# Gram matmuls of a DLRM tower, moved from blocks of their own to the places between other matmuls

## What is computed

```
e = jnp.stack([tbl_0[ids[:, 0]], ..., tbl_25[ids[:, 25]]], axis=1)
combined = jnp.concatenate([dense_features[:, None, :], sparse_features], axis=1)
interactions = jnp.einsum('bnd,bmd->bnm', combined, combined)
interactions_flat = interactions[:, _TRIU_I, _TRIU_J]
z = jnp.concatenate([dense_features, interactions_flat], axis=1)
h = jnp.concatenate([z, r_dense_features], axis=1)
h = jnp.maximum(h @ W_top1 + b_top1, 0.0)
h = jnp.maximum(h @ W_top2 + b_top2, 0.0)
y = h @ W_top3
```

## Time and profile before

| | |
|---|---|
| median of 3 runs | 381.85 us (380.86 to 382.14) |
| the profiled execution | 384.91 us, span 382.8 us |
| TensorE matmuls busy | 341.9 us (89%) |
| TensorE weight loads busy | 304.2 us (79%) |
| GpSimd busy | 252.1 us (66%) |
| VectorE, ScalarE busy | 193.2 us, 125.5 us |
| granted TensorE clock, mean | 0.99 of full |

### The profile page before, as it was taken

The page is one execution under the profiler, slowest core; times in us unless marked ns, Lnnn a source line. Parts: engine busy times, 40 slices in busy tenths (PEclk is TensorE's granted clock), DMA queues, the critical chain, the costliest instruction groups (busy, mean ns, idle before and its releaser), DMA issues.

```text
span 382.8 us, 13108 instructions
## 1 busy us (share of the span) xinstructions
PE 341.9 (89%) x6048; PEld 304.2 (79%) x6048; DVE 193.2 (50%) x94; ACT 125.5 (33%) x211; POOL 252.1 (66%) x267
## 2 busy tenths in 40 slices
PE   0788878984999999999999999999999999999995
PEld 0687767883898898898988898889988898977763
DVE  2899996565424396228833495238742595100000
ACT  2235433332132341334322342323322333343122
POOL 3777887777777777777777777777777777500200
PEclk9999999999799999999999999999999999999999
DMA  8975698254322537225632536234622533420400
GB/s 205 222 210 166 170 301 250 58 195 126 126 80 58 193 82 200 58 80 177 149 119 58 194 92 190 58 120 140 187 79 58 193 89 86 144 73 27 154 13 0
DMA packets 30868, 49.57 MB, mean 129 GB/s; under 512 B 17499, under 2 KB 17635, under 8 KB 30686
## 3 DMA queue, kind: packets, MB, share of 16 engines
q1 hardware_dynamic: 22350, 31.68, 27.0%
q0 software_dynamic: 8320, 16.92, 16.8%
q10 hardware_dynamic: 144, 0.13, 0.1%
HBM read 38.21 MB, written 10.49 MB: 127 GB/s over the span
## 4 chain that ended last, share of the span: by engine, by line
PE 72%; POOL 14%; issue 6%; DMA 4%; DVE 2%; ACT 1%; DVEq 0%
PE look_ps L309 28%; POOL rows L290 14%; PE mid_ps L339 13%; PE layer_ps L356 11%; PE layer_ps L365 7%; PE mid_ps L321 7%; PE layer_ps L353 4%; DMA rows<-in_table,index 3%; DVE match L463 2%; PE layer_ps L372 2%; DMA index<-in_index 1%; ACT hidden L528 0%; ACT hidden L534 0%; ACT turned L501 0%; ACT turned L512 0%
## 5 line engine op out<-in xcount | busy, mean ns | idle before, releaser
L290 POOL DMA_INDIRECT rows<-in_table,index x256 | 248.8, 972 | 82.3 <-issue 75.0
L463 DVE TENSOR_TENSOR match<-look_ids,row_number_ps 125x2048 fp32r<-125x2048 int32 x80 | 181.7, 2286 | 132.2 <-PE look_ps L309 122.3
L309 PE MATMUL look_ps<-match,table_high 125*128 125x256 f32 x640 | 165.7, 296 | 20.2 <-DVE table_low L471 18.1
L309 PE MATMUL look_ps<-match,table_low 125*128 125x256 f32 x640 | 159.4, 286 | 0.1
L309 PEld LDWEIGHTS look_ps<-match,table_high 125*128 125x128 f32 x640 | 124.8, 195 | 25.0 <-issue 16.0
L309 PEld LDWEIGHTS look_ps<-match,table_low 125*128 125x128 f32 x640 | 125.1, 195 | 0.0
L339 PEld LDWEIGHTS mid_ps<-turned 128*32 128x32 f32 x4096 | 45.3, 109 | 19.1 <-issue 15.3
L339 PE MATMUL mid_ps<-turned 128*32 128x27 f32 x4096 | 54.4, 195 | 5.5 <-issue 1.7
L501 ACT COPY turned<-look_ps 128x512 f32<-128x512 f32 x40 | 31.9, 798 | 73.5 <-PE look_ps L309 72.2
L508 ACT COPY turned<-mid_ps 128x512 f32<-128x512 f32 x64 | 42.8, 672 | 19.7 <-PE mid_ps L321 19.5
L321 PE MATMUL mid_ps<-identity,rows 128*128 128x128 f32 x256 | 40.6, 283 | 9.4 <-DMA rows<-in_table,index 8.5
(11 more groups left out here) (21 smaller groups left out, 44.8 us busy)
## 6 DMA issues: line engine op xcount, KB each, us to landing
look_ids<-in_look_rows SPq DMA_DIRECT2D x40, 256.0 KB, 4.4
scratch<-grams SPq DMA_DIRECT2D x8, 864.0 KB, 4.4
rows<-in_table,index POOLq DMA_INDIRECT x256
scratch<-grams SPq DMA_DIRECT2D x8, 416.0 KB, 5.2
pairs<-scratch SPq DMA_DIRECT2D x92, 29.2 KB
grams<-in_table SPq DMA_DIRECT2D x4, 448.0 KB
pairs<-in_table SPq DMA_DIRECT2D x3, 448.0 KB
hidden<-in_table SPq DMA_DIRECT2D x3, 448.0 KB
```

Of the source, the lines that this page charges most:

```text
L290: pool.indirect_dma_start(out=rows[j % 2][:, at, :], out_offset=None, in_=tables[GATHERED[at]], in_offset=bass.IndirectOffsetOnAxis(ap=ind ...
L309: last = nc.tensor.matmul(look_ps[pair % 2][:, r % 2, :], part[0:table_rows, r, c, :], match[number % 2][0:table_rows, c, :], start=(c == ...
L463: nc.vector.tensor_tensor(match[number % 2][0:table_rows], look_ids[b][0:table_rows, r % 2].unsqueeze(1).broadcast_to(shape), row_number_p ...
```

## The change

28 of the 32 gram steps (all but the four of the last group) lose their block. `look` takes a gram step along and sets four samples behind every matmul, or behind every second one (`every=2`); `layer1` and `layer2` take four samples behind each of their matmuls. In the main loop from g = 2, steps 0, 1 and 2 are half in a look and half in layer 1 or layer 2; step 3 stands whole in a look. The steps of group 0 and of group 6 stand whole in looks. The numbers of the shared PSUM banks follow the new order (each turn now ahead of its gram step), and so does ScalarE's order. In the last group's tail the blocks of gram and of the layers change places.

```diff
+            def look(g, r, step=None, every=1):
                 ...
+                if step is not None:
+                    gram_ready(g - 1, step)
                 for c in range(PARTS):
-                    for part in (table_high, table_low):
+                    for h, part in enumerate((table_high, table_low)):
                         last = nc.tensor.matmul(look_ps[pair % 2][:, r % 2, :], part[0:table_rows, r, c, :],
                         ...
-                last.then_inc(look_done, 1)
+                        if c == PARTS - 1 and part is table_low:
+                            last.then_inc(look_done, 1)
+                        if step is not None and (2 * c + h + 1) % every == 0:
+                            four_samples(g - 1, step, (2 * c + h) // every)
...
+            def four_samples(g, k, i):
+
+                x = k * IN_STEP + i
+                for s in range(QUADS):
+                    n = (x // BLOCK * P + s * BLOCK + x % BLOCK) * FEATURES
+                    last = nc.tensor.matmul(
+                        mid_ps[gram_number(g, k) % 3][s * ROW:(s + 1) * ROW, i * FEATURES:(i + 1) * FEATURES],
+                        turned[g % 2][:, n:n + ROW], turned[g % 2][:, n:n + FEATURES], start=True, stop=True)
+                if i == IN_STEP - 1:
+                    last.then_inc(gram_done, 1)
...
+            turn(1, 0)
+            look(1, 6, step=0)
...
-                gram(g - 1, 0)
-                turn(g, 0)
-                look(g, 6)
-                if g >= 2:
-                    layer1(g - 2, 0)
-                    layer1(g - 2, 1)
...
+                    turn(g, 0)
+                    look(g, 6, step=0, every=2)
+                    layer1(g - 2, 0, grams=(g - 1, 0, 8))
+                    layer1(g - 2, 1, grams=(g - 1, 0, 12))
...
+                    turn(g, 2)
+                    look(g, 8, step=2, every=2)
+                    layer2(g - 2, grams=(g - 1, 2, 8))
+                    turn(g, 3)
+                    look(g, 9, step=3)
                     layer3(g - 2)
...
             for k in range(STEPS):
-                gram(g - 1, k)
                 turn(g, k)
-                look(g, AHEAD + k)
+                look(g, AHEAD + k, step=k)
             layer1(g - 2, 0)
             layer1(g - 2, 1)
             gram(g, 0)
             layer1(g - 2, 2)
+            layer1(g - 2, 3)
             gram(g, 1)
...
+            layer2(g - 2)
+            for k in range(STEPS, TURNS):
+                turn(g, k)
             gram(g, 2)
-            layer2(g - 2)
+            layer3(g - 2)
             gram(g, 3)
-            layer3(g - 2)
```

More of the change, by code:

```diff
@@ L161, in pair_end, with mid_order @@
             return 2 * number + 2
-        PERIOD = TURNS + STEPS
-        def turn_number(g, k):
[L169 to L174, removed]
+        def mid_order():
+            yield from (("turn", 0, k) for k in range(TURNS))
+            for g in range(1, groups):
+                for k in range(STEPS):
+                    yield "turn", g, k
+                    yield "gram", g - 1, k
+                if g + 1 < groups:
+                    yield from (("turn", g, k) for k in range(STEPS, TURNS))
+            yield from (("gram", g, 0), ("gram", g, 1))
+            yield from (("turn", g, k) for k in range(STEPS, TURNS))
+            yield from (("gram", g, 2), ("gram", g, 3))
+        mid_place = {step: number for number, step in enumerate(mid_order())}
+        def turn_number(g, k):
+            return mid_place["turn", g, k]
         def gram_number(g, k):
[L177 to L180, removed]
+            return mid_place["gram", g, k]
         block = ctx.enter_context(nc.Block())
@@ L323, in turn, with gram_ready @@
                 last.then_inc(turn_done, 1)
-            def gram(g, k):
-                number = gram_number(g, k)
+            def gram_ready(g, k):
                 if k == 0:
@@ L333, in gram, with layer1 @@
                     pe.wait_ge(mid_out, turn_number(g, TURNS - 1) + 1)
-                after(pe, mid_out, number - 2)
-                for i in range(IN_STEP):
[L336 to L344, removed]
+                after(pe, mid_out, gram_number(g, k) - 2)
+            def four_samples(g, k, i):
[7 more added lines that the diff above has]
+                    last.then_inc(gram_done, 1)
+            def gram(g, k):
+                gram_ready(g, k)
+                for i in range(IN_STEP):
+                    four_samples(g, k, i)
+            def layer1(g, o, grams=None):
                 if o == 0 and g + 1 < groups:
@@ L354, in layer1 @@
                                  dense[:, g * N:(g + 1) * N], start=True, stop=False)
+                if grams is not None:
+                    four_samples(*grams)
                 for c in range(CHUNKS):
@@ L357, in layer1, with layer2 @@
                                             pairs[0:CHUNK_ROWS, g % 2, c, :], start=False, stop=(c == CHUNKS - 1))
-                if o % 2 == 1:
-                    last.then_inc(layer1_done, 1)
-            def layer2(g):
+                    if c == CHUNKS - 1 and o % 2 == 1:
+                        last.then_inc(layer1_done, 1)
+                    if grams is not None:
+                        of, k, first = grams
+                        four_samples(of, k, first + 1 + c)
+            def layer2(g, grams=None):
                 pe.wait_ge(hidden1_ready, L1 * (g + 1))
@@ L366, in layer2 @@
                                                 start=(c == 0), stop=(c == L1 - 1))
-                last.then_inc(layer2_done, 1)
+                        if o == L2 - 1 and c == L1 - 1:
+                            last.then_inc(layer2_done, 1)
+                        if grams is not None:
+                            of, k, first = grams
+                            four_samples(of, k, first + o * L1 + c)
             def layer3(g):
@@ L390, in _ @@
             pe.wait_ge(dense_in, 16)
+            turn(1, 0)
+            look(1, 6, step=0)
+            turn(1, 1)
+            look(1, 7, step=1)
+            turn(1, 2)
+            look(1, 8, step=2)
+            turn(1, 3)
+            look(1, 9, step=3)
             for g in range(1, groups - 1):
@@ L394, in _ @@
                     pe.wait_ge(weights_in, WEIGHT_DMAS)
-                gram(g - 1, 0)
-                turn(g, 0)
-                look(g, 6)
                 if g >= 2:
-                    layer1(g - 2, 0)
-                    layer1(g - 2, 1)
-                gram(g - 1, 1)
-                turn(g, 1)
-                look(g, 7)
-                if g >= 2:
[L405 to L410, removed]
-                    layer2(g - 2)
[L412 to L415, removed]
+                    turn(g, 0)
+                    look(g, 6, step=0, every=2)
+                    layer1(g - 2, 0, grams=(g - 1, 0, 8))
+                    layer1(g - 2, 1, grams=(g - 1, 0, 12))
+                    turn(g, 1)
+                    look(g, 7, step=1, every=2)
+                    layer1(g - 2, 2, grams=(g - 1, 1, 8))
+                    layer1(g - 2, 3, grams=(g - 1, 1, 12))
+                    turn(g, 2)
[3 more added lines that the diff above has]
+                    look(g, 9, step=3)
                     layer3(g - 2)
@@ L592, in _ @@
             g = groups - 1
+            take_turned(g, 0)
             take_gram(g - 1, 0)
-            take_turned(g, 0)
+            take_turned(g, 1)
             take_gram(g - 1, 1)
-            take_turned(g, 1)
             take_look(g, 3)
-            take_gram(g - 1, 2)
             take_turned(g, 2)
             put_dense(g)
+            take_gram(g - 1, 2)
+            take_turned(g, 3)
             take_gram(g - 1, 3)
-            take_turned(g, 3)
             take_look(g, 4)
@@ L605, in _ @@
             take_gram(g, 0)
+            relu1(g - 2, 1)
             take_gram(g, 1)
[L607 to L611, removed]
+            relu2(g - 2)
+            for k in range(STEPS, TURNS):
+                take_turned(g, k)
             take_gram(g, 2)
-            relu2(g - 2)
+            copy_y(g - 2)
             take_gram(g, 3)
-            copy_y(g - 2)
             for g in (groups - 2, groups - 1):
```

15 lines of the change are left out of this document (4 added, 11 removed).

## The result

The changed kernel takes 549.06 us in the median (545.08 to 551.04), the kernel before 381.93 us: 1.437 times as long, 95% interval 1.428 to 1.446. That is +167 us where +101 was forecast, and beyond the range's 525. The profiled execution took 550.15 us, with a span of 548.3 us.

What follows compares the result with a forecast made beforehand. From about 97 us TensorE's own queue was taken to bound the kernel, GpSimd's gathers close behind. Pieces 165.8, removed blocks -54.3, hidden -10 and -1, tail +0.4 made +100.9 us on the 381.85 median: 483 us, range 445 to 525.

Steps and rivals of the forecast that it cites:

- rival 2: Next wide weights load during the piece, so 0.11 us of its exit goes: 0.26 us a piece, 433 us; chance 5%.
- A piece: Four samples set among look or layer matmuls, entry, matmuls and exit together: 0.37 us each, 165.8 us for 448.
- The exit into a look: Passage from a piece's gram matmuls back to a look matmul, taken like layer 1's: 0.23 us.
- layer matmuls about 0.59 us: Sign of being right: layer matmuls on either side of a piece stand about 0.59 us apart.
- the clock falls: Spread pieces leave TensorE's array mostly empty; all at the lower level 703 us, a fifth 527; chance 7% beyond 525.
- A main-loop group: Sign of being right: TensorE's period of a main-loop group goes from 42.3 to 58.2 us.
- what is hidden: In group 0's stretch, 57 to 103 us, added grams fill idle time and end slow clock: 10 us off.
- VectorE's match waits: TensorE's waits for VectorE's matches go: another 1 us off.
- the tail: Layer 3 of group 5 moves ahead of the last gram and no longer covers the chain to pairs: +0.4 us.
- Rival 1: Pieces cost array time alone, spreading may avoid pauses inside blocks: -23 us, capped by gathers at about 369 us; chance 6%.

Runs made afterwards that it cites:

- r5: Changed kernel with one gram matmul of 32 weight columns in each of the 448 pieces instead of four: 540.79 us.
- r6: Changed kernel with one gram matmul of 128 weight columns in each piece instead of four narrow ones: 427.02 us, and 447 us three times.
- r1: Changed kernel's order, but each of the 28 gram steps is one piece of sixteen four-samples behind its look: 386.43 us.
- r3: Changed kernel's order, but each gram step is eight pieces of two four-samples, behind every second look matmul: 431.2 us in its two faster executions.
- r4: Changed kernel with the 13 gram steps that stood behind every single look matmul put back into blocks: 447.01 us.
- r9: Changed kernel with only group 0's four gram steps put back into blocks: 517.15 us.
- r10: As r9, with each look matmul done twice in the remaining 9 looks with a piece behind every matmul: 503.37 us.
- r2: Changed kernel's order, but each gram step is two pieces of eight four-samples, behind the 8th and 16th look matmul: 389.34 us.
- r7: Changed kernel with each look matmul done twice in the 13 looks that have a piece behind every matmul: 547.53 us.
- r12: Kernel before, with gram steps 0 and 1 joined, and 2 and 3 joined next to layer 3: 418.7 us in its three faster executions.

## Why the prediction was wrong

**Right: the sign and the mechanism.** Wide and narrow weights cost a passage each time they meet (r5 against r6, r1 to r3), the next wide weights are not loaded ahead (rival 2 is out), and the pieces are nearly all passage. The direction had a chance of 92%.

**Right: the size at the full clock.** A piece was put at 0.37 us; the trace has 0.39 in looks (0.51 - 0.12) and 0.40 in layer 1. The exit into a look, the largest unknown, was as dear as the one into layer 1. That is +8 us on 448 pieces. r4, which has no slow clock to speak of, came within 2 us of a sum with such pieces. The sign "layer matmuls about 0.59 us" left out that a layer matmul is two instructions: by the prediction's own terms it is 0.43 + 0.37 = 0.80, and 0.83 was measured.

**Wrong: the clock.** The step that failed is "the clock falls" as a rival with 7% beyond 525 us, and the sum's assumption of a full clock. The prediction knew one fall, behind 4.26 us of idle time, and expected no such idle time. r9 and r10 show that a stretch without idle time loses the clock with a piece behind every look matmul, and keeps it with two look matmuls to a piece. By the trace, 145 of the 448 pieces ran at the lower level and took 0.77 instead of 0.51 us with their look matmul, 38 us; the other 36 us spent at that level (148 less 145 x 0.77) would have been about half as long at the full clock, some 18 us less, and 4 go off for the 7 us that the kernel before had. That makes an estimate of 52 us of the 66 by which the forecast fell short. A second estimate, from r4, is 47 us: 447 us and 13 x (16 x 0.387 - 1.94) = 55 for the steps that r4 has in blocks are 502 us at the full clock, and 549 was measured. A main-loop group takes 62.2 us (L369 starts at 260.93 and 323.11) where 58.2 was forecast. The rival gave a look matmul and its piece 0.98 us at the lower level, too much, and let a fifth of the pieces run there for 527 us; it was a third.

**Wrong: what is hidden.** 10 us were taken off for idle time and slow clock between 57 and 103 us. TensorE's waits for rows fell from 8.5 to 4.8 us only, since turn(1, 0) now comes ahead of the gram step that used to fill that wait, and the slow clock there did not end but stayed for 54 us. This is +4 us of idle time, and the clock's part is in the sum above. The 1 us for VectorE's match waits did not go either (0.9 us after, 0.7 before).

**Wrong by a little: the tail.** +0.4 us was forecast for the order; r1 has it at +4, some of it slow clock, most of it pauses in narrow blocks that now stand closer. Together 52 + 8 + 4 + 1 + 3 and the 3 us of slow clock that the forecast had removed make 71, against 64 missing in the profiled executions (550.15 less 486): the terms overlap, and the sum is 7 us too large.

**Rival 1, faster.** Its one true point, the pauses, is there: 4 us in r2, and at most the 16 us that the prediction counted when every pause goes, less than the passages that any spreading needs.

## What to carry to other kernels

Count how often consecutive matmuls change between 128 weight columns and 32: here each change and the way back cost 0.31 to 0.33 us, nearly as much as three look matmuls, so small narrow matmuls belong in blocks of their own. Blocks have an upper size as well: runs of 16 narrow matmuls with their loads had no pause (r3), most of 64 (r2) and nearly all of 128 had, and two blocks of 128 joined took 4.7 to 8.3 us instead of 3.6. And when an edit thins out the wide matmuls in a stretch, price it at both levels of the clock; here a busy share of 100% in the trace did not tell one from the other.

## What the runs showed of the hardware

- The clock fell to its lower level with TensorE busy all the time by its records, where one 256-column matmul stood in 0.51 us, and held with two in 0.63 us. Whether the rarer wide matmuls or the denser passages do it was not separated. Adding 144 matmuls made a kernel 14 us faster (r9, r10).
- Once low, it stayed low in a stretch with two look matmuls to a piece (r7, 59 to 134 us) in which it did not fall by itself elsewhere in the same run. "TensorE: Matmul & The Clock Gate" of the Trainium skill, Part 1, says that the default is throttled and activity releases it; the trace agrees, and shows besides that what held the full clock did not regain it in r7, in all four executions (clock 0.93).
- A gram matmul with 128 weight columns cost less between wide matmuls (0.22 us in layer 1, r6) than one with 32 (0.37 us, r5).
- Long runs of narrow matmuls pause with no semaphore in sight: 1.10 us from first to last matmul for a block of 128 at best, 7.4 us for one of 256 in r12. The 15 pauses of over 1 us in r12 all end 1.3 to 1.5 us after a 16 KB transfer of instructions. Why the supply falls behind there was not settled; the pauses grow with the length of the narrow run (r12) and shrink with wide work between (r2).
